# A decoder layer on one core: the mask and bias of the attention rows in one VectorE operation, the row products on GpSimd, and later tiles turned by DMA

## The reference, cut to what matters

```python
q = rmsnorm(x @ w_qa, q_norm_w) @ w_qb         # 16 heads, 128 + 64 rotary
kv = x @ w_kva                                 # latent 128, rotary key 64
scores = einsum('blhd,bmhd->bhlm', q, k) * scale
scores = where(tril, scores, -1e30)
attn = softmax(scores, axis=-1)
out = einsum('bhlm,bmhd->blhd', attn, v)
return out.reshape(B, L, H * DV) @ w_o
```

## Time and profile before

| | us |
|---|---|
| three runs | 1168.90, 1169.56, 1170.61 |
| median | 1169.56 |
| span of the profiled execution | 1169.4 |
| TensorE busy | 980.4 (84%) |
| VectorE busy | 959.2 (82%) |
| ScalarE busy | 678.1 (58%) |
| GpSimd busy | 296.4 (25%) |

### The profile page before, as it was taken

How to read it: one execution, slowest core, us unless ns; L and a number is a source line. 1 busy time by engine, 2 the same in 40 slices (tenths; PEclk the granted TensorE clock), 3 DMA queues, 4 the chain that set the end, 5 groups by cost and what they waited for, 6 DMA issues and landing times.

```text
span 1169.4 us, 18715 instructions
## 1 busy us (share of the span) xinstructions
PE 980.4 (84%) x6106; PEld 574.0 (49%) x6124; DVE 959.2 (82%) x2669; ACT 678.1 (58%) x1449; POOL 296.4 (25%) x524
## 2 busy tenths in 40 slices
PE   0446667899999999999999999999978655559997
PEld 0234444555555555555555555555545544435553
DVE  5757749989989888989998988888868898866885
ACT  1446557667667666756666666656512676754442
POOL 1036533223223223222322222213100113221211
PEclk9769779999999999999999999999989888769999
DMA  9300003433323336334335244336363520001333
GB/s 350 139 1 1 1 8 73 75 59 71 71 59 67 66 62 142 62 64 69 65 68 138 55 68 60 64 67 140 68 218 86 168 91 19 0 1 36 84 80 91
DMA packets 217328, 90.78 MB, mean 78 GB/s; under 512 B 191496, under 2 KB 202760, under 8 KB 216720
## 3 DMA queue, kind: packets, MB, share of 16 engines
q1 hardware_dynamic: 217232, 89.58, 33.5%
HBM read 36.06 MB, written 7.34 MB: 37 GB/s over the span
## 4 chain that ended last, share of the span: by engine, by line
PE 53%; DVE 30%; ACT 6%; issue 5%; POOL 3%; DMA 3%; SPq 0%; DVEq 0%; ACTq 0%; POOLq 0%
PE bank L1930 13%; PE bank L1880 8%; PE bank L1915 6%; PE bank L1828 3%; PE bank L1859 3%; DVE arena L709 2%; PE bank L1898 2%; DVE arena L711 2%; PE bank L1901 2%; PE bank L1899 2%; PE bank L1900 2%; PE bank L1902 2%; DVE arena L791 2%; DVE arena L675 2%; DVE arena L1529 2%
## 5 line engine op out<-in xcount | busy, mean ns | idle before, releaser
L1218 ACT ACTIVATE arena<-bank,arena,scal 128x128 f32<-128x128 f32 (+3 forms) x256 | 157.7, 616 | 112.7 <-POOL arena L1059 111.6
L1930 PE MATMUL bank<-arena 128*128 128x512 f16 x768 | 179.1, 381 | 1.9 <-DVE arena L1562 1.9
L1536 DVE SCALAR_TENSOR_TENSOR arena<-arena 128x128 f16<-128x128 f32 (+3 forms) x256 | 142.2, 555 | 9.1
L1059 POOL TENSOR_TENSOR arena<-arena,scal 128x1 f32<-128x1 f32 x256 | 51.7, 203 | 347.4 <-DVE arena L1512 345.7
L1880 PE MATMUL bank<-arena 128*128 128x512 f16 x576 | 137.6, 385 | 0.0
L1529 DVE TENSOR_SCALAR arena<-arena 128x128 f16<-128x128 f32 (+3 forms) x256 | 125.4, 490 | 7.4 <-DVE arena L1521 0.8
L1512 DVE TENSOR_REDUCE arena<-bank 128x1 f32<-128x128 f32 (+3 forms) x256 | 123.7, 483 | 7.8 <-PE bank L1903 6.7
L1915 PE MATMUL bank<-arena 128*128 128x512 f16 (+3 forms) x768 | 117.7, 304 | 11.5 <-DMA arena<-arena 5.8
L1930 PEld LDWEIGHTS bank<-arena 128*128 128x128 f16 x768 | 72.9, 98 | 81.0 <-issue 4.4
L1915 PEld LDWEIGHTS bank<-arena 128*128 128x128 f16 x768 | 71.8, 99 | 63.0 <-issue 16.5
L1237 ACT ACTIVATE arena<-bank 32x512 f32<-32x512 f32 x128 | 75.3, 588 | 26.0 <-PE bank L1859 24.7
(11 more groups left out here) (201 smaller groups left out, 2049.5 us busy)
## 6 DMA issues: line engine op xcount, KB each, us to landing
arena<-in_L_attn_w_qb SPq DMA_DIRECT2D x1, 4608.0 KB, 21.6
arena<-arena SPq DMA_TRANSPOSE x272, 2.7
arena<-in_x SPq DMA_DIRECT2D x4, 1024.0 KB, 6.9
arena<-in_L_attn_w_o SPq DMA_DIRECT2D x1, 4096.0 KB, 31.9
arena<-in_fside_BxS2xS SPq DMA_DIRECT2D x4, 1024.0 KB, 8.8
arena<-in_L_ffn_w SPq DMA_DIRECT2D x8, 512.0 KB, 7.6
out<-arena SPq DMA_DIRECT2D x16, 256.0 KB, 2.3
arena<-in_x SPq DMA_DIRECT2D x12, 256.0 KB, 3.0
```

The source lines that it names most:

```text
L1218: act.activation(pf(k), banks[S_BANKS[G % 3]][:, 0:n], ACT.Exp, bias=NB[:, k:k + 1], scale=sc_exp, accum_out=SUM[:, k:k + 1]).then_inc(s_e ...
L1536: dve.scalar_tensor_tensor(out=ph_part(k, 1), in0=pf(k).rearrange("p (t c) -> p t c", c=P), scalar=R4[:, k:k + 1], in1=ph_part(k, 0), op0= ...
L1930: last = pe.matmul(banks[Y_BANK][:, :], ot(gp, a, k, (q & 3) * P, P), wo(b, gp * GH + k), start=(k == 0 and n == 0), stop=(k == GH - 1 and ...
```

## The change

- The mask's table is as wide as a row (512, zeros ahead of the last 128 columns). TensorE's sixth matmul goes. VectorE's `row_max` becomes one `tensor_tensor_reduce`: it adds the mask, multiplies by the negated scale, writes the result back into the bank and gives the row's minimum, which is the bias. ScalarE's exponential takes it directly, with scale -1, and waits for VectorE instead of GpSimd. GpSimd's `bias` goes.
- `row_scale` is the reciprocal alone and stands ahead of the next tile's `row_max`. GpSimd's new `row_unit` multiplies it by 4096, at the head of each g of its list, where `bias` was, for tile g - 1.
- The probabilities of k = 2 are kept in rows of 136 instead of 128, of which 128 are used.
- Tiles 4 to 15 are turned by three DMA transposes on SP: the rows' halves (`turn_rows`), the keys (`turn_keys`) and the latents (`turn_latents`), straight to where `prep_te` and `prep_out` had copied them. TensorE's transposes, ScalarE's copy and VectorE's two copies go for these tiles, and with them the wait of `rope_mm` for the keys' copy.

The core of the diff (the waits of `prep_hi`, `prep_rope` and `prep_split` change from the transposes to the DMAs in the same way, and `row_scale` leaves every place of VectorE's list):

```diff
@@ -249,7 +251,11 @@
                 :, 0:2 * (k + 1), k * P:(k + 1) * P]
 
         def pf(k):
-            return PF[:, k * (k + 1) // 2 * P:(k + 1) * (k + 2) // 2 * P]
+
+            o = (0, P, 3 * P, 6 * P + 24)[k]
+            if k == 2:
+                return PF[:, o:o + 3 * (P + 8)].rearrange("p (t c) -> p t c", c=P + 8)[:, :, 0:P]
+            return PF[:, o:o + (k + 1) * P].rearrange("p (t c) -> p t c", c=P)
 
         def ph(k):
             return PH[:, k * (k + 1) * P:(k + 1) * (k + 2) * P]
...
@@ -1011,9 +1017,32 @@
                     sp.wait_ge(pv_mm, Hd - 1)
                 sp.dma_start_transpose(pt_blocks(g >> 2, k), ph(k)).then_inc(pt_in[k], 16)
 
+            def turn_rows(n):
+
+                sp.wait_ge(xn_lo, n + 1)
+                sp.wait_ge(kv_mm, n)
+                sp.dma_start_transpose(XNT.rearrange("p (a q) -> p a q", a=8), XH).then_inc(xn_in, 16)
+
+            def turn_keys(n):
+
+                sp.wait_ge(kr_made, n + 1)
+                sp.dma_start_transpose(part_kr((n >> 2) & 1, n & 3), KN).then_inc(kr_in, 16)
+
+            def turn_latents(n):
+
+                sp.wait_ge(ch_lo, n + 1)
+                sp.dma_start_transpose(part_ct((n >> 2) & 1, n & 3), CH).then_inc(ct_in, 16)
+
             load_xt(TB)
+            turn_rows(TB)
             for i in range(NPAIR):
                 for g in range(8):
+                    if i % 2 == 1 and g == 6 and i // 2 + 5 < NT:
+                        turn_rows(i // 2 + 5)
+                    if i % 2 == 0 and g == 3 and i // 2 + TB < NT:
+                        turn_keys(i // 2 + TB)
+                    if i % 2 == 0 and g == 4 and i // 2 + TB < NT:
+                        turn_latents(i // 2 + TB)
                     turn_probs(i, g)
                     if g == 3 and i % 2 == 0 and i // 2 + 5 < NT:
                         load_xt(i // 2 + 5)
...
@@ -1052,11 +1082,11 @@
                 pool.wait_ge(sv_made, n + 1)
                 pool.tensor_tensor(srq, sv, half[:, 0:2], ALU.pow).then_inc(srq_pow, 1)
 
-            def bias(G, g):
-
-                pool.wait_ge(s_max, G + 1)
-                k = g & 3
-                pool.tensor_tensor(NB[:, k:k + 1], NEGM[:, k:k + 1], sc_exp, ALU.mult).then_inc(s_bias, 1)
+            def row_unit(G):
+
+                k = G & 3
+                pool.wait_ge(s_rc, G + 1)
+                pool.tensor_tensor(R4[:, k:k + 1], RC[:, k:k + 1], pscale, ALU.mult).then_inc(s_r4, 1)
 
             def rope_sin(i):
 
@@ -1077,7 +1107,8 @@
             def pair(i, j, first=False, last=False, prep=None, ahead=None):
                 G = 8 * i
                 for g in range(8):
-                    bias(G + g, g)
+                    if not (first and g == 0):
+                        row_unit(G + g - 1)
                     if (j, g) == (0, 2):
                         if prep is not None:
                             prep_norm(prep[0])
...
@@ -1178,7 +1210,9 @@
 
             def prep_hi(n):
                 act.wait_ge(xn_made, n + 1)
-                if not (n == 0):
+                if n > TB:
+                    act.wait_ge(xn_in, 16 * (n - TB))
+                elif n > 0:
                     act.wait_ge(xn_t, n)
                 act.activation(XH[:, 0:D], XN, ACT.Copy).then_inc(xn_hi, 1)
 
@@ -1212,10 +1246,11 @@
             def exps(G, g):
                 k = g & 3
                 n = (k + 1) * P
-                act.wait_ge(s_bias, G + 1)
+                act.wait_ge(s_max, G + 1)
                 if not (G < 4):
                     act.wait_ge(s_lo, G - 3)
-                act.activation(pf(k), banks[S_BANKS[G % 3]][:, 0:n], ACT.Exp, bias=NB[:, k:k + 1], scale=sc_exp,
+                act.activation(pf(k), banks[S_BANKS[G % 3]][:, 0:n].rearrange("p (t c) -> p t c", c=P), ACT.Exp,
+                               bias=NB[:, k:k + 1], scale=-1.0,
                                accum_out=SUM[:, k:k + 1]).then_inc(s_exp, 1)
 
             def out_hi(Hd):
...
@@ -1254,8 +1289,6 @@
                 for g in range(8):
                     exps(G + g, g)
                     if (j, g) == (0, 0):
-                        if prep is not None:
-                            prep_te(prep[0])
                         qn_hi_(2 * i + 1, 1)
                     if (j, g) == (0, 1):
                         if prep is not None:
...
@@ -1489,8 +1525,11 @@
 
             def prep_split(n):
                 dve.wait_ge(cf_made, n + 1)
-                if not (n == 0):
+                if n > TB:
+                    dve.wait_ge(ct_in, 16 * (n - TB))
+                elif n > 0:
                     dve.wait_ge(ct_t, n)
...
@@ -1509,16 +1548,15 @@
 
                 n = ((g & 3) + 1) * P
                 dve.wait_ge(s_mm, G + 1)
-                dve.tensor_reduce(NEGM[:, (g & 3):(g & 3) + 1], banks[S_BANKS[G % 3]][:, 0:n], AX.X, ALU.max,
-                                  negate=True).then_inc(s_max, 1)
+                s = banks[S_BANKS[G % 3]][:, 0:n]
+                dve.tensor_tensor_reduce(s, s, maskb[:, L - n:L], nsc_exp, 3e38, ALU.add, ALU.min,
+                                         NB[:, (g & 3):(g & 3) + 1]).then_inc(s_max, 1)
 
             def row_scale(G, g):
 
                 k = g & 3
                 dve.wait_ge(s_exp, G + 1)
                 dve.reciprocal(RC[:, k:k + 1], SUM[:, k:k + 1]).then_inc(s_rc, 1)
-                dve.wait_ge(s_rc, G + 1)
-                dve.tensor_scalar(R4[:, k:k + 1], RC[:, k:k + 1], PSCALE, None, ALU.mult).then_inc(s_r4, 1)
 
             def probs_hi(i, g):
 
@@ -1526,14 +1564,14 @@
                 dve.wait_ge(s_r4, G + 1)
                 if not (i == 0 and g < 4):
                     dve.wait_ge(pt_in[k], 16 * (2 * i + (g >> 2)))
-                dve.tensor_scalar(ph_part(k, 0), pf(k).rearrange("p (t c) -> p t c", c=P), R4[:, k:k + 1], None,
+                dve.tensor_scalar(ph_part(k, 0), pf(k), R4[:, k:k + 1], None,
                                   ALU.mult).then_inc(s_hi, 1)
 
             def probs_lo(G, g):
 
                 k = g & 3
                 dve.wait_ge(s_hi, G + 1)
-                dve.scalar_tensor_tensor(out=ph_part(k, 1), in0=pf(k).rearrange("p (t c) -> p t c", c=P),
+                dve.scalar_tensor_tensor(out=ph_part(k, 1), in0=pf(k),
                                          scalar=R4[:, k:k + 1], in1=ph_part(k, 0), op0=ALU.mult,
                                          op1=ALU.subtract).then_inc(s_lo, 1)
 
@@ -1565,36 +1603,33 @@
             def pair(i, j, first=False, last=False, prep=None, ahead=None):
                 G = 8 * i
                 for g in range(8):
+                    if not (first and g == 0):
+                        row_scale(G + g - 1, g - 1)
                     row_max(G + g, g)
                     if (j, g) == (0, 0):
                         if not first:
-                            row_scale(G - 1, 7)
                             probs_hi(i - 1, 7)
                             probs_lo(G - 1, 7)
                             out_lo(2 * i - 2)
                     if (j, g) == (0, 1):
-                        row_scale(G, 0)
                         probs_hi(i, 0)
...
@@ -1565,36 +1603,33 @@
             def pair(i, j, first=False, last=False, prep=None, ahead=None):
                 G = 8 * i
                 for g in range(8):
+                    if not (first and g == 0):
+                        row_scale(G + g - 1, g - 1)
                     row_max(G + g, g)
...
                     if (j, g) == (0, 6):
-                        row_scale(G + 5, 5)
-                        if prep is not None:
-                            prep_out(*prep)
                         probs_hi(i, 5)
                         probs_lo(G + 5, 5)
...
@@ -1819,7 +1841,10 @@
             def prep_mm(n):
 
-                pe.wait_ge(xn_te, n + 1)
+                if n < TB:
+                    pe.wait_ge(xn_te, n + 1)
+                else:
+                    pe.wait_ge(xn_in, 16 * (n - TB) + 16)
...
@@ -1899,8 +1929,7 @@
-                pe.matmul(bank[:, 0:n], qr(j, 2, q, P), kr(bp, 1 + h, 0, n), start=False, stop=False)
-                pe.matmul(bank[:, q:n], identb[:, :], maskb[:, :], start=False, stop=True).then_inc(s_mm, 1)
+                pe.matmul(bank[:, 0:n], qr(j, 2, q, P), kr(bp, 1 + h, 0, n), start=False, stop=True).then_inc(s_mm, 1)
...
@@ -1938,8 +1967,6 @@
-                        if prep is not None:
-                            prep_t(prep[0])
...
@@ -1955,9 +1982,6 @@
-                    if (j, g) == (0, 6):
-                        if prep is not None:
-                            prep_t2(prep[0], i + 1)
```

More of the change, by code:

```diff
@@ L104, in decoder_layer @@
         RT1 = take(L)
-        PF = take(10 * P)
+        PF = take(10 * P + 24)
         PH = take(20 * P, fp16)
@@ L132, in decoder_layer @@
         small = take(40)
-        NEGM, NB, SUM, RC, R4 = (small[:, 20 + 4 * k:24 + 4 * k] for k in range(5))
+        NB, SUM, RC, R4 = (small[:, 20 + 4 * k:24 + 4 * k] for k in range(4))
         rstd = small[:, 10:11]
```

(31 more changed lines are left out.)

35 lines of the change are left out of this document (13 added, 22 removed).

## The result

The changed kernel takes 1206.09 us (median of four runs, 1203.8 to 1206.81) against 1170.09 before: 1.030 times as long (95% interval 1.0283 to 1.0318), 36 us more. Forecast were 1179 us and a range of 1156 to 1197. The direction was right; the size was wrong and the result lies outside the range.

A forecast was written before the change was run, and what follows sets the result against it. TensorE was taken to bound the loop, busy 44.48 of 44.66 us per period. Relief of 29.1 us against 38.4 us of new waits gave +9.3 on 1169.4: forecast 1179 us, range 1156 to 1197.

The forecast's parts named there:

- Row 3 behind the sine product: Even pairs: GpSimd makes row 3's scale behind the sine product, so TensorE waits 2.4 us before values(i, 0).
- The price of that wait: TensorE's wait before values in sixteen even pairs, 2.4 us each, adds 38.4 us to the time.
- The clock could be read before: TensorE's clock was said to stand at its upper level, 2.4 GHz, all through the attention loop, 185 to 853 us.
- the two idle times: First four pairs: TensorE already idles 1.86 us before scores(1, 0) and again before scores(3, 0); effect left at nothing.
- What TensorE gets back: TensorE's queue in the loop loses the mask matmuls and twelve later tiles' transposes: together 29.1 us.
- DMA turning: Transposes of the twelve later tiles leave TensorE: 12 x 1.25 = 15.0 us; the rows' turning by DMA costed at nothing.
- the mask matmuls: TensorE: 256 mask matmuls go, each delaying the next by 0.055 us: 14.1 us.
- Costs on VectorE: New row minimum costs 0.1 us more per row, 1.6 per period: 37.4 of 44.7 us, fitting the slack.
- Rival C: VectorE becomes the bound if the new minimum costs over 0.26 us more per row; at 0.33, 1197 us; chance 0.09.
- The distances: Rotary matmuls, even pair to next odd one about 20.7 us apart instead of 19.49, odd to even 24.2 instead of 25.17.
- Rival A: TensorE's relief reaches the end, the stall before values being covered: 1140 us, or 1160 with half the stall; chance 0.21.
- forecast case: The even pairs' stall of 2.1 to 2.7 us outweighs TensorE's relief: 1173 to 1187 us; chance 0.58.

The follow-up runs named there:

- the filler run: Changed kernel with ten extra 512-column matmuls, results thrown away, on TensorE ahead of the even pairs' first values; 1187.58 us, ratio 1.0147.
- the best kernel: Changed kernel with GpSimd making row 3's scale product ahead of the rotary sine product in even pairs; 1143.23 us, ratio 0.9766.
- mask alone: Kernel before with only mask, scale and bias put in VectorE's minimum; mask matmul and GpSimd's bias go; 1194.52 us, ratio 1.0212.
- transposes on TensorE again: Changed kernel with the later tiles transposed on TensorE as before, GpSimd's order left as changed; 1202.61 us, ratio 1.0279.
- row product alone: Kernel before with only the row product moved to GpSimd, behind the next row's bias; 1224.61 us, ratio 1.0447.
- the last run: Kernel before with mask, scale and bias in VectorE's minimum, plus two GpSimd waits keeping its sine product and sum behind VectorE's splits; 1165.35 us, ratio 0.996.

## Why the prediction was wrong, by its own steps

- **Row 3 behind the sine product: right**, in place, cause and count. Sixteen waits, one in each even pair; GpSimd's product directly behind the sine product; VectorE's idle time 2.41 for 2.4; TensorE comes to `values` 8.11 us behind the rotary matmuls, as worked out, and the turned row 10.74 behind them for 10.56, its DMA landing 3.4 us after the issue and not 3.0.
- **The price of that wait: the step that failed.** The prediction put 16 x 2.4 = 38.4 us. The waits are 46.0 (2.6 to 2.7 in pairs 2 to 20, 2.95 to 3.66 in the later ones, 3.63 in pair 0): 7.6 off. And it priced a microsecond of idle time at a microsecond. From 180 us to the loop's end TensorE had eleven stretches of 3.4 us at its lower level more than before (15 for 4), 1.66 us each, 18.3 in all, a term that wasn't in the sum; the filler run removes eleven and gets some 18 us back. The 36 us less these 46.0 and 18.3 leave -28.3, where the relief was put at -29.1.
- **The clock could be read before.** The prediction says that it stands at its upper level all through the loop; it read tenths of slices of 29 us. The kernel before has two low stretches between 185 and 853 us, from 228.4 us behind a wait of 1.86 that ends at 227.10 (the second of the two idle times that the forecast names with the earlier trace rows), and from 245.4 behind one of 2.61. The first of them:

```profile
228.40:231.80 3.40, 3.40 (x11) 1.20 (x9) 3.26 (x9) 1.45 (x5) 0.19 (x1) 0.51 0.40 63
```

- **What TensorE gets back: 29.1 predicted, 27.4 measured** (the best kernel, 0.0234 x 1170), but the sum came out better than its parts. DMA turning gives 6 to 7 us there (1149.91 less 1143.23) instead of 15.0. The rest, some 20, comes with the other parts, where 14.1 was put on the mask matmuls. In mid-loop they give what was forecast (1.03 us per period, with the wait of 0.18); the other few us come in the early pairs and in single pairs where the kernel before waits longer (1.20 us at 478.31), for which the forecast put nothing. That the two errors nearly cancel is luck. Of the 36 us, 2 are lost up to the rotary matmuls of pair 5, 15 from there to pair 23 and 14 from there to pair 31: the last pairs have no transposes to save and longer waits.
- **Costs on VectorE: right enough.** The new minimum takes 745 ns at 512 against 686, so 0.06 where 0.1 was taken. The split of 384 takes 482 ns. A period with transposes has 37.19 us of VectorE work (37.4 forecast). Neither is felt, as forecast. Rival C has nothing for it (VectorE 76%). Its reciprocal waits for the exponential more than the forecast's "mostly is over": 58.8 us in all, 16.4 before.

```profile
L1552 DVE CUSTOM_DVE_ANT_0 bank<-bank,maskb,scal 128x512 f32<-128x512 f32 x63 | 46.9, 745 | 0.3 <-PE bank L1932 0.3
...
L1552 DVE DVE_READ_ACCUMULATOR2_ANT arena<- 128x1 f32 x250 | 35.6, 142 | 0.0
...
L1567 DVE TENSOR_SCALAR arena<-arena 128x384 f16<-128x384 f32 x63 | 30.4, 482 | 1.4
```

- **The distances:** from the rotary matmuls of an even pair to those of the next odd one 20.9 us without and 22.6 with the low clock (20.7 forecast), odd to even 24.6 (24.2 forecast, 25.17 before). The clock explains the first (22.6); the second misses by a wait of 0.2 for `add_y` and by less relief.
- **Rival A** (1140 without the stall) is the kernel with one instruction moved: 1143.2. It didn't come about in the changed kernel, but its number holds.
- The range ended at 1197 because its upper end was made for rival C. The forecast case's own upper end, 1187, and the clock's 18.3 make 1205, one us under the result.

## What to carry to other kernels

A small operation on an in-order queue costs what stands ahead of it, not what it takes: look for the place where its consumer needs it, and issue it ahead of the long one. When a change adds a wait to an engine that is otherwise always busy, price the wait and, apart from it, what the granted clock does behind it; a run with filler matmuls tells the two apart. Before crediting or blaming an edit, look whether VectorE's operations that read and write SBUF kept their length, those with two inputs first: a shift of 0.2 us against GpSimd can cost more than the edit brings.

## What the runs showed of the hardware

- Between 257 and 842 us, behind the changed kernel's waits of 2.63 to 2.67 us six of nine times a stretch of 3.4 us at 0.50 of the clock, behind those of 2.95 us and more four of four times. Waits of 2.0 us had one in 20 of 30 cases (mask alone 8 of 10, transposes on TensorE again 7 of 10, row product alone 5 of 10). Behind waits of up to 1.8 us there was none, but neither was there behind one of 2.51, and at the start of the loop one of 1.86 had one. So the length of the wait alone doesn't decide; what does isn't settled.
- VectorE against GpSimd: an operation with two SBUF inputs that starts with, or within 0.3 us behind the start of, a GpSimd product of 1.3 to 1.4 us ends 0.55 us behind that product: 1.82 us for 0.75, 1.64 for 0.69. Kept apart, both are back at their length. It is not only two inputs: the copy of the latents to fp16 (one input) takes 0.42 alone, 1.12 beside the sine product in the last run, and 0.90 already in the kernel before (533.04, 1.04 behind the start of the sine product). The Trainium skill (GPSIMD Engine Reference, 1. Specifications) says that the two engines share their SBUF interfaces and contend when VectorE's operation has two SBUF inputs or runs in a 2-port perf mode; the runs agree on the first, and add the size. Whether the copy runs in such a mode no row shows.
- The reduction with an accumulator is two records, 745 ns at 512 and a read of 142 ns. By the Trainium skill (VectorE: DVE Perf Modes, Two Vector instructions with no wait between them) such an operation is two instructions; the rows agree. In the timeline the first runs from 399.05 to 399.81 and the read starts at 399.73, so most of its 142 ns isn't added.
